# A graph network kernel on one core: 1,722 gathers of h rows are given the last row as a bound, with indices over it skipped

## The chip, the cores and the metric

The kernel runs on one core of one Trainium2 chip. The metric is the device time of one execution in microseconds (us). The time before the change is 3790.28 us, the median of two runs (3790.26 and 3790.29).

## What is computed

The input is x, 6250 nodes by 256 features, and 100,000 edges (src, dst) sorted by dst. Six graph layers are followed by a mix term and a mixture of eight experts:

```python
xn = _layernorm(x)
h = xn
for layer in range(6):
    agg = segment_sum(h[src], dst, num_segments=n)
    z = h + agg
    z = relu(batchnorm(z @ W1[layer] + b1[layer]))
    z = batchnorm(z @ W2[layer] + b2[layer])
    h = z if layer == 5 else relu(z)
x = x + h + mix(xn)
x = x + experts(_layernorm(x))
```

The step that matters here is `segment_sum(h[src], dst)`: for each node, the sum of the rows of h at the other ends of its edges.

## The kernel before, in words

The 6250 nodes are cut into 13 chunks by destination. The first 8 chunks (510 nodes each) are done densely: an adjacency matrix of edge counts, a "slab" of 49 tiles of 128 source nodes by 510 destinations, is multiplied with h, which stays in SBUF as two fp16 pieces (`PC`, named pieces). These are 8 x 196 matmuls a layer on TensorE at line 1181. The slabs are built in layer 0 and loaded again from memory by SyncE in each later layer.

The other 5 chunks are done sparsely, by "slots". A slot is 128 edges that follow one another in the sorted list. There are 287 of them (`NSLOT`). For each slot GpSimd issues one indirect DMA, a gather at line 1518: it takes 128 indices from one column of `SI` (named ssrc) and fetches 128 rows of 512 fp16 values, 1 KB each, from `d_H` (pieces_d), the copy of h in memory, into a buffer `SG` (sg0 to sg9, and from layer 1 on also sgm0 to sgm3). VectorE builds a one-hot matrix `SO` for the slot (line 1899), and TensorE multiplies gathered rows by it in 4 short matmuls (line 1217), which wait for the gather's semaphore `s_row` and the one-hot's `s_soh`. The last one counts up `s_smm`, and that frees the buffer. The indices in `SI` come from src with `min(N - 1)` applied (N is 6250), so none is over 6249.

The order of the work is written out ahead by `layer_order` and `side_work`: 1568 dense steps a layer, and at given steps a slot's matmuls. All engines follow the same list `ORDER[l]`, each for the items that concern it. Among the slots' matmuls stand mostly 5 dense matmuls. GpSimd runs ahead of TensorE: item `fetch_first` issues the first `lead_of(l)` gathers of the layer (8 in layer 0, 12 after it) once the writes of h to `d_H` have landed (`s_hst`), and each later gather j is issued in the order of slot j - `lead_of(l)`, after a wait on `s_smm` until its buffer, one of a ring of `ring_of(l)` (10 in layer 0, 14 after it), is free. GpSimd does nothing else while the gathers of layers 1 to 5 run. In layer 0 it also has a few operations for the slab keys among them.

After the last slot of a layer come the remaining dense steps, the statistics, the second matmul of the layer (lines 2067 and 2149), the scaling of h (line 1406) and its write to `d_H`, and the next layer's gathers. After layer 5 come the experts, with no such gathers.

The change touches `pool_layer` alone. Line 1076 (`pool_start`) holds ten other gathers of the same instruction, at the start of the program, three of them with 96 indices and seven with 128. The gathers inside `general` (line 2266) are for inputs that the fast path can't take, and don't run here.

Of the kernel before, what the change touches and what calls it, by code (L numbers as in the profile page):

```python
# [15 lines left out]
N = 6250  # L16
# [79 lines left out]
def ring_of(l):  # L96
    return RINGS + MORE if l else RINGS

def lead_of(l):  # L100
    return ring_of(l) - 2
# [197 lines left out]
def product_count(l, q, i, m):  # L299

    return gemm_count(l, q, i, m) - 2 * NCH * l
# [158 lines left out]
def build(nc, inp, cst, out):  # L460
# [33 lines left out]
    def small(name, shape, dt):  # L494
        return at(name, shape, dt, region(nbytes(shape, dt)))
# [11 lines left out]
    SI = small("ssrc", [P, 3 * SROWS], I32)  # L507
# [164 lines left out]
    def ring(name, k):  # L672
        return [nc.alloc_semaphore(f"{name}{i}") for i in range(k)]
# [15 lines left out]
    s_xin, s_xst, s_row = ring("s_xin", 4), ring("s_xst", 4), ring("s_row", RINGS + MORE)  # L689
# [360 lines left out]
    def pool_keys(w):  # L1050
        hi, lo = phl[w % 2][:, 0, :], phl[w % 2][:, 1, :]
        r, b, c, d = (pkt[j][:, :] for j in range(4))
        pool.wait_ge(s_bits, w)
        pool.wait_ge(s_kk, w + 2)
        pool.tensor_scalar(b, hi, float(WD), 1.0, ALU.mult, ALU.add)
        pool.tensor_scalar(r, GE_T[w][:, 0:256], wb5[:, w:w + 1], None, ALU.subtract).then_inc(s_pl, 1)
        pool.wait_ge(s_pl, pn())
        pool.tensor_scalar(c, r, 0.0, None, ALU.is_ge)
        pool.tensor_scalar(d, r, float(WD - 1), None, ALU.is_le)
        pool.tensor_tensor(b, b, r, ALU.add).then_inc(s_pl, 1)  # L1060
        pool.wait_ge(s_pl, pn())
        pool.tensor_scalar(r, lo, 1.0, None, ALU.add)
        pool.tensor_tensor(c, c, d, ALU.mult).then_inc(s_pl, 1)
        pool.wait_ge(s_pl, pn())
        pool.tensor_tensor(b, b, c, ALU.mult)
        pool.tensor_tensor(r, r, c, ALU.mult).then_inc(s_pl, 1)
        pool.wait_ge(s_pl, pn())
        pool.wait_ge(s_turn, w + 3)
        pool.tensor_tensor(pkk[:, 0, :], b[:, 0:P], b[:, P:2 * P], ALU.add)
        pool.tensor_tensor(pkk[:, 1, :], r[:, 0:P], r[:, P:2 * P], ALU.add).then_inc(s_kk, 1)  # L1070
# [327 lines left out]
    def pool_y(l):  # L1398
        pool.wait_ge(s_bn, norm_count(l - 1, 1))
        for g, (c, w) in enumerate(YG):  # L1400
            pool.wait_ge(s_gev, y_done(l, g))
            for m in range(2) if g else (1,):
                n = 2 * g + m
                if n >= YRING:
                    pool.wait_ge(s_ylo, 2 * len(YG) * (l - 1) + n - YRING + 1)
                pool.tensor_scalar(RY[n % YRING][:, 0:w], Z[:, m, c:c + w], scaled[:, m, 0:1], scaled[:, m, 1:2],  # L1406
                                   ALU.mult, ALU.add).then_inc(s_yf, 1)
# [91 lines left out]
    def pool_layer(l):  # L1499
        for item in ORDER[l]:  # L1500
            kind, i = item[0], item[1] if len(item) > 1 else None
            if kind == "bits":
                pool_keys(i)
            elif kind == "y" and i == 0:
                pool_y(l)
            elif kind == "fetch_first" or kind == "fetch":
                if kind == "fetch_first":
                    pool.wait_ge(s_hst, 16 * (9 + 14 * l))
                    if l == 0:
                        pool.wait_ge(s_keys, 4)  # L1510
                        pool.wait_ge(s_xst[3], 32)
                    else:
                        pool.wait_ge(s_gemm, product_count(l - 1, 1, NG2 - 1, 1))
                        pool.wait_ge(s_smm, NSLOT * l)
                for j in range(lead_of(l)) if kind == "fetch_first" else (i,):
                    if j >= ring_of(l):
                        pool.wait_ge(s_smm, NSLOT * l + j - ring_of(l) + 1)
                    pool.indirect_dma_start(out=SG[j % ring_of(l)][:, :], out_offset=None, in_=d_H[:, :],  # L1518
                                            in_offset=bass.IndirectOffsetOnAxis(ap=SI[:, j:j + 1], axis=0)
                                            ).then_inc(s_row[j % ring_of(l)], 16)  # L1520

    def sp_layer(l):
        for item in ORDER[l]:
# [1175 lines left out]
    def rest(any_edges):  # L2699

        for l in range(L):
            if l:
                pe_layer(l)
                act_layer(l, any_edges)
                dve_layer(l, any_edges)
                pool_layer(l)
                sp_layer(l)
            if any_edges:
                general(l)
            if l == L - 1:  # L2710
                sp_tail()
            pe_second(l)
            act_second(l, not any_edges)
            dve_second(l, not any_edges)
            pool_second(l)
        pe_ffn()
        act_ffn()
        dve_ffn()
        pool_ffn()
        sp_ffn()  # L2720
# [7 lines left out]
    act_layer(0)  # L2728
    dve_layer(0)
    pool_layer(0)  # L2730
    sp_layer(0)
    for engine in (pe, dve, act, pool, sp):
# [74 lines left out]
```

## Time and profile before

| | |
|---|---|
| runs | 3790.26 and 3790.29 us, median 3790.28 |
| the profiled execution, first to last instruction (its span) | 3784.5 us |
| runs over the span: what lies around it | 5.8 us |
| granted TensorE clock, mean | 0.997 |
| TensorE matmul busy | 96% |
| VectorE, ScalarE, GpSimd busy | 56%, 37%, 73% |
| gathers at line 1518 | 1,722 (6 x 287) |
| matmuls at line 1217 | 6,888 (4 for each gather) |

The profile gives no own time for the profiled execution beyond its span, so the 5.8 us are the runs' median less the span. PE is TensorE, DVE is VectorE, ACT is ScalarE, POOL is GpSimd, SP is SyncE. A gather's row on POOL lasts as long as POOL works on issuing it, and not until the rows have landed. Instructions of the sequencers (semaphores, registers) aren't counted as busy. "idle <-X" is time in which an engine did nothing, ended by X; "issue" means that nothing in the profile held it. A busy PE isn't PE at its peak, since matmuls overlap.

### The profile page before, as it was taken

How to read it: one execution, taken by the hardware profiler on the slowest of the kernel's cores; microseconds unless marked ns; L12 is line 12 of the kernel's file. 1: busy time of each engine (PE TensorE's matmuls, PEld its weight loads, DVE VectorE, ACT ScalarE, POOL GpSimd, SP SyncE). 2: the span in 40 equal slices, each digit the busy share in tenths (PEclk: the TensorE clock that was granted, in tenths of full speed). 3: DMA queues.
4: the chain of work that ended last, by engine and by line, in shares of the span. 5: the costliest groups of instructions: out<-in, count | busy, mean ns of one | idle time of the engine just before them, and what ended most of it. 6: DMA issues, size and time to landing. Idle time of an engine off the chain costs nothing.

```text
span 3784.5 us, 69343 instructions
## 1 busy us (share of the span) xinstructions
PE 3634.5 (96%) x26358; PEld 2033.4 (54%) x26358; DVE 2109.3 (56%) x6775; ACT 1416.3 (37%) x2665; POOL 2756.0 (73%) x2845
## 2 busy tenths in 40 slices
PE   2899999999999999999999999999999999999999
PEld 1455554544456555555555555555554555665666
DVE  9988775556465444732227222282223776777766
ACT  6666654200042000510006000060001767677777
POOL 5666664677756777667776677667776799999997
PEclk9999999999999999999999999999999999999999
DMA  6444342668525555255552565535554100000000
GB/s 205 144 127 151 124 151 84 204 220 273 177 100 185 190 173 172 90 186 192 193 182 95 170 207 181 169 128 189 190 177 126 63 22 12 23 12 23 11 16 10
DMA packets 203707, 506.19 MB, mean 134 GB/s; under 512 B 33860, under 2 KB 137872, under 8 KB 196848
## 3 DMA queue, kind: packets, MB, share of 16 engines
q0 software_dynamic: 83360, 227.95, 20.3%
q1 hardware_dynamic: 120016, 273.74, 19.9%
q8 instruction: 218, 3.57, 0.4%
q14 instruction: 113, 0.93, 0.1%
HBM read 412.08 MB, written 89.48 MB: 133 GB/s over the span
## 4 chain that ended last, share of the span: by engine, by line
PE 77%; DVE 9%; ACT 4%; DMA 4%; issue 3%; POOL 3%; SPq 0%; POOLq 0%; ACTq 0%; DVEq 0%
PE bank L1181 47%; PE bank L2428 6%; PE bank L2411 6%; PE bank L2396 5%; PE bank L1217 4%; PE bank L1293 3%; DMA sg<-pieces_d,ssrc 2%; PE bank L983 2%; DVE zh L2167 1%; ACT h L2467 1%; ACT f L2468 1%; DVE st L2192 1%; POOL sg L1518 1%; DVE ohk L782 1%; POOL ry L1406 1%
## 5 line engine op out<-in xcount | busy, mean ns | idle before, releaser
L1181 PE MATMUL bank<-slab,pieces 128*128 128x510 fp8e4 (+1 forms) x9408 | 2321.0, 378 | 5.3 <-DVE slab L801 5.3
L1518 POOL DMA_INDIRECT sg<-pieces_d,ssrc x1322 | 1261.7, 954 | 548.8 <-issue 249.4
L1181 PEld LDWEIGHTS bank<-slab,pieces 128*128 128x128 f16 (+1 forms) x9408 | 800.8, 97 | 668.2 <-DVE slab L801 7.7
L1899 DVE TENSOR_SCALAR so<-iota,skey 128x49 f16<-128x49 f16 (+21 forms) x1322 | 319.1, 262 | 599.5 <-PE bank L1217 598.2
L1423 ACT ACTIVATE z<-bank,prm,ct 128x510 f32<-128x510 f32 (+2 forms) x130 | 94.9, 749 | 1223.2 <-DVE st L1417 1223.2
L1217 PEld LDWEIGHTS bank<-so,sg 128*128 128x128 f16 x5288 | 322.1, 96 | 286.5 <-DMA sg<-pieces_d,ssrc 14.7
L1518 POOL DMA_INDIRECT sgm<-pieces_d,ssrc x400 | 380.7, 952 | 121.8 <-issue 90.8
L2686 POOL TENSOR_SCALAR btmp<-bob,rw 128x256 f32<-128x256 f32 (+1 forms) x343 | 400.3, 1167 | 33.5
L2467 ACT ACTIVATE h<-bank,fscale 128x512 f16<-128x512 f32 (+2 forms) x416 | 314.8, 757 | 186.4 <-PE bank L2411 186.1
L1217 PE MATMUL bank<-so,sg 128*128 128x51 f16 (+20 forms) x5288 | 343.2, 182 | 9.3 <-DMA sg<-pieces_d,ssrc 9.2
L930 ACT ACTIVATE slab<-bank 128x490 fp8e4<-128x490 f32 x408 | 278.4, 695 | 141.3 <-PE bank L983 138.1
L2468 ACT ACTIVATE f<-bank,fscale 128x512 f32<-128x512 f32 (+2 forms) x416 | 316.2, 760 | 0.0
L2689 POOL TENSOR_TENSOR mb<-mb,btmp 128x256 f32<-128x256 f32 (+1 forms) x343 | 279.6, 815 | 28.6
L2428 PE MATMUL bank<-fwo,h 128*128 128x256 f16 (+1 forms) x2352 | 277.9, 273 | 6.4 <-DVE h L2533 4.8
L2411 PE MATMUL bank<-h,fw 128*128 128x512 f16 (+2 forms) x1248 | 274.0, 367 | 6.6 <-ACT h L2467 3.8
L2396 PE MATMUL bank<-xp,fw 128*128 128x512 f16 (+2 forms) x1248 | 271.9, 366 | 0.3 <-ACT xp L2510 0.3
L983 PE MATMUL bank<-ohk,ohl 128*128 128x245 f16 x816 | 220.5, 284 | 44.7 <-ACT slab L930 33.5
L2428 PEld LDWEIGHTS bank<-fwo,h 128*128 128x128 f16 (+1 forms) x2352 | 227.1, 98 | 58.7 <-DVE h L2533 10.9
L782 DVE TENSOR_SCALAR ohk<-iota,keys 128x245 f16<-128x245 f16 x816 | 251.9, 311 | 0.0
L781 DVE TENSOR_SCALAR ohl<-iota,keys 128x128 f16<-128x128 f16 x816 | 228.1, 280 | 7.9 <-PE bank L983 4.8
L2533 DVE TENSOR_TENSOR h<-f,h 128x512 f16<-128x512 f32 (+2 forms) x208 | 145.8, 701 | 128.7 <-ACT f L2468 126.7
L1417 DVE BATCH_NORM_STATS2 st<-bank 128x6 f32<-128x510 f32 (+2 forms) x130 | 84.0, 662 | 229.4 <-PE bank L1181 136.9
(355 smaller groups left out, 3946.0 us busy)
## 6 DMA issues: line engine op xcount, KB each, us to landing
slab<-slabs SPq DMA_DIRECT2D x40, 3123.8 KB
pieces_d<-pieces SPq DMA_DIRECT2D x60, 512.0 KB
slabs<-slab SPq DMA_DIRECT2D x8, 3123.8 KB, 11.9
sg<-pieces_d,ssrc POOLq DMA_INDIRECT x1322
mx<-xnorm SPq DMA_DIRECT2D x24, 512.0 KB
ws<-L_ffn_W_dram SPq DMA_DIRECT2D x32, 256.0 KB, 8.1
sgm<-pieces_d,ssrc POOLq DMA_INDIRECT x400
experts<-wp SPq DMA_DIRECT2D x24, 256.0 KB, 4.1
```

The source lines that it names most:

```text
L782: dve.tensor_scalar(OHK[w % RING][:, 0:KW], iota[:, 0:KW], KL[:, 0, w:w + 1], None, ALU.is_equal).then_inc(s_oh, 1)
L983: pe.matmul(win_bank(pr)[:, KW * u:KW * u + KW], OHL[w % RING][:, :], OHK[w % RING][:, 0:KW], start=True, stop=True).then_inc(s_bmm, 1)
L1181: ins = pe.matmul(psD[half][:, 0:w], PC[:k, a, c:c + P], v[:k, a, :], start=(r == 0), stop=(r == 97))
L1217: ins = pe.matmul(psS(l)[half][:, lo:lo + w], SG[i % ring_of(l)][:, c:c + P], SO[i % ring_of(l)][:, 0:w], start=False, stop=True, skip_gro ...
L1518: pool.indirect_dma_start(out=SG[j % ring_of(l)][:, :], out_offset=None, in_=d_H[:, :], in_offset=bass.IndirectOffsetOnAxis(ap=SI[:, j:j + ...
L1899: dve.tensor_scalar(SO[j % ring_of(l)][:, 0:w], iota[:, 0:w], SK[:, j:j + 1], None, ALU.is_equal).then_inc(s_soh, 1)
L2396: ins = pe.matmul(psD[m][:, 0:n], fw1[:, e, k, pw, P * m:P * m + P], xps[c % 2][:, k, px, 0:n], start=(j == 0), stop=(j == 5))
L2411: ins = pe.matmul(psG[m][:, 0:n], fw2[:, e, k, pw, P * m:P * m + P], h1[:, k, px, 0:n], start=(j == 0), stop=(j == 5))
L2428: ins = pe.matmul(psB[pr][:kr, 256 * u:256 * u + 256], h2[:, k, px, P * (i0 + u):P * (i0 + u) + kr], fwo[:, e, k, pw, :], start=(j == 0), ...
L2467: act.activation(h[:, m, 0, 0:n], ps[m][:, 0:n], ACT.Relu, bias=b_, scale=s_).then_inc(s_h, 1)
L2468: act.activation(f[m][:, 0:n], ps[m][:, 0:n], ACT.Relu, bias=b_, scale=s_).then_inc(s_f, 1)
L2686: pool.tensor_scalar(btmp[:k, :], bob[e][:k, :], w_[:k, i, e:e + 1], None, ALU.mult).then_inc(s_pl, 1)
```

## The change

```diff
                     pool.indirect_dma_start(out=SG[j % ring_of(l)][:, :], out_offset=None, in_=d_H[:, :],
-                                            in_offset=bass.IndirectOffsetOnAxis(ap=SI[:, j:j + 1], axis=0)
-                                            ).then_inc(s_row[j % ring_of(l)], 16)
+                                            in_offset=bass.IndirectOffsetOnAxis(ap=SI[:, j:j + 1], axis=0),
+                                            bounds_check=N - 1, oob_is_err=False).then_inc(s_row[j % ring_of(l)], 16)
```

Each gather of line 1518 now names row 6249 as the last that may be read, and a row whose index is over it is left out of the transfer. No index is over it, so the same 128 rows are fetched. The list of instructions on each engine is the same before and after, row for row (PE 11830, DVE 10147, ACT 3092, POOL 5352, SP 628 rows). That list doesn't show register instructions.
## Rows read from the trace of the kernel before

**Rows 1.** The page: busy time of each engine, and the chain that ended last.
```profile
PE 3634.5 (96%) x26358; PEld 2033.4 (54%) x26358; DVE 2109.3 (56%) x6775; ACT 1416.3 (37%) x2665; POOL 2756.0 (73%) x2845
...
PE 77%; DVE 9%; ACT 4%; DMA 4%; issue 3%; POOL 3%; SPq 0%; POOLq 0%; ACTq 0%; DVEq 0%
```

**Rows 2.** Line 1518: durations (ns min/median/max), and POOL's idle time before it.
```profile
L1518 POOL DMA_INDIRECT sg<-pieces_d,ssrc x1322: 940/946/4613, 142.1 to 2905.7; - x189
L1518 POOL DMA_INDIRECT sgm<-pieces_d,ssrc x400: 942/946/1493, 713.3 to 2896.9; - x134
its engine sat idle before it (us, times) until:
  issue: 340.1, 1117
  PE bank L1217: 255.8, 600
  DMA pieces_d<-pieces: 74.7, 5
```

**Rows 3.** Timeline of POOL: first and last gathers of layer 0, then of layer 5.
```profile
142.12 1.09 POOL L1518 DMA_INDIRECT sg<-pieces_d,ssrc  x1 [0.16 <-issue]
...
573.77 0.94 POOL L1518 DMA_INDIRECT sg<-pieces_d,ssrc  x1 [0.31 <-issue]
...
2547.80 0.98 POOL L1518 DMA_INDIRECT sg<-pieces_d,ssrc  x1 [14.70 <-DMA pieces_d<-pieces]
...
2905.66 0.95 POOL L1518 DMA_INDIRECT sg<-pieces_d,ssrc  x1 [0.30 <-issue]
```

**Rows 4.** Timeline of PE in layer 5: the first and the last slot's matmuls.
```profile
2558.30 0.24 PE L1217 MATMUL bank<-so,sg 128*128 128x14 f16 x4
2558.41 1.24 PE L1181 MATMUL bank<-slab,pieces 128*128 128x510 fp8e4 x5
...
2916.42 0.25 PE L1217 MATMUL bank<-so,sg 128*128 128x32 f16 x4
2916.52 5.77 PE L1181 MATMUL bank<-slab,pieces 128*128 128x510 fp8e4 x26
```

**Rows 5.** Line 1518 in the gather stretches of layers 1 and 5: span, POOL busy (instructions).
```profile
700.00:1084.00 384.00, 274.88 (x287) 0.99 0.66 215
...
2547.00:2918.00 371.00, 271.67 (x287) 1.00 0.54 173
```

**Rows 6.** Line 1217, all layers: PE's idle time before it, by what ended it.
```profile
  DMA sg<-pieces_d,ssrc: 23.9, 21
  DMA sgm<-pieces_d,ssrc: 10.1, 9
```

**Rows 7.** Waits of POOL in layer 0 (142 to 700 us): total us, times, longest.
```profile
POOL sg L1518 <- PE bank L1217: 134.4, 220, 7.2
```

**Rows 8.** DMA issues of the page: a load from memory and its median time to landing.
```profile
mb<-mixed SPq DMA_DIRECT2D x10, 512.0 KB, 3.9
```

**Rows 9.** The chain that ended last, its longest DMA pieces in layers 2 and 5.
```profile
1210.73 10.82 DMA sg<-pieces_d,ssrc
...
2587.83 10.73 DMA sg<-pieces_d,ssrc
```

**Rows 10.** Waits of POOL in layer 5 (2547 to 2922 us): total us, times, longest.
```profile
POOL sg L1518 <- issue: 48.8, 160, 0.3
...
POOL sg L1518 <- PE bank L1217: 14.0, 46, 0.3
```

**Rows 11.** Timeline of POOL: two operations of which the second needs the first.
```profile
65.68 0.40 POOL L1055 TENSOR_SCALAR pkt<-phl 128x256 f32<-128x256 int32 x1 [4.38 <-DVE phl L790]
66.16 0.93 POOL L1056 TENSOR_SCALAR pkt<-ge,cf 128x256 f32<-128x256 int32 x1
```

**Rows 12.** Line 1076: gathers with 128 indices, and with 96 indices (ns min/median/max).
```profile
L1076 POOL DMA_INDIRECT ge<-edges_dram,cwi x7: 946/953/1160, 14.7 to 26.1; - x7
L1076 POOL DMA_INDIRECT ge<-slot_edges_dram,cwi x3: 909/912/926, 16.2 to 18.7; - x3
```

## The prediction

> **What bounds the kernel now.** I read the page first. PE is busy for 96% of the span and makes up 77% of the chain that ended last, and POOL is busy for 73% and makes up 3% of the chain [rows 1]. By that alone, some more work on POOL would be hidden. But these are averages over the program, so I next read the one line that the change touches. A gather keeps POOL busy for 0.946 us at the median, and before nearly each one POOL is idle: 1117 times for 340.1 us in all until "issue" (0.30 us each), 600 times for 255.8 us until PE's slot matmuls, and 5 times until the copy of h has landed, once in each of layers 1 to 5 [rows 2]. "Issue" says that nothing held POOL. So 0.95 + 0.30 = 1.25 us is what a gather costs POOL from start to start, and a gather that starts 1.25 us after the one before it was held up by nothing.
>
> The timeline shows where that is so. In layer 5 the first gather starts at 2547.80 and the last, the 287th, at 2905.66: 357.9 us for 286 steps, or 1.251 us a step [rows 3]. POOL never stops there. TensorE goes through the same slots at the same pace: from 2558.30 to 2916.42 is 358.1 us, or 1.252 us a slot [rows 4]. Two engines with one pace, and POOL's pace is its own cost. Layers 1 to 5 are alike, 287 gathers each in 384 us (layer 1) to 371 us (layer 5) [rows 5]; layer 1 is the loosest, by 13 us. The order gives PE mostly 5 dense matmuls and a slot's 4 per slot. PE hardly waits for the gathers: 23.9 + 10.1 = 34 us over all layers [rows 6]. So in this stretch PE is busy, but only just: POOL is 100% taken with no reserve beyond what is in flight. In layer 0 it is otherwise. Its gathers take from 142.12 to 573.77, 431.7 us or 1.509 us a step [rows 3], and POOL waits 134.4 us for buffers [rows 7], so PE sets the pace there and POOL has 1.509 - 1.25 = 0.26 us to spare per gather.
>
> How much is in flight: the first gather of layer 5 ends at 2548.78 and its matmuls start at 2558.30, 9.5 us later. The last ends at 2906.61 and is used at 2916.42, 9.8 us later [rows 3, 4]. Part of that is the landing. The trace has no landing time for gathers by itself. A 512 KB load lands in 3.9 us [rows 8], and a gather moves 128 KB, so I take 4 us for a common one; but in each of layers 2 to 5 the chain runs once through a gather that took over 10 us to land (10.82 and 10.73 in layers 2 and 5 [rows 9]), and leaves no reserve there. The reserve s is thus between 0 and 9.8 - 4 = 5.8 us. I take 5, since a late landing must fall near the layer's end to take it away.
>
> **The change, part by part.** It removes and moves nothing, and adds two things to each of 1,722 gathers. Say they cost POOL d us per gather together. Then the last gather of a layer comes 286 d later, its slot waits for it, and behind that slot are only 26 dense matmuls, 5.77 us [rows 4], before the layer's statistics. PE works in order, so the layer grows by 286 d - s. Nothing gives it back: the next layer's h, its copy to memory and its gathers all start from this end. Over layers 1 to 5 that is 5 (286 d - s).
>
> First, the register write. It sits on POOL's sequencer ahead of the gather. It costs nothing if the sequencer does it while the gather before is still being worked on. For that speaks that in layer 5 the idle time is the same whether it is ended by "issue" (48.8 us over 160, 0.30) or by the matmul that frees the buffer (14.0 over 46, 0.30) [rows 10]. Against it speaks the same 0.30 us: between dependent ordinary operations POOL loses only 66.16 - 66.08 = 0.08 us [rows 11], so something in a gather's start doesn't overlap. The ends are 0 and 0.30 (a whole second start of a gather), nearest is the 0.08 of the hand-over, and I take 0.05.
>
> Second, the test of 128 indices against the bound. Without a test, 128 indices take 0.953 us and 96 take 0.912 [rows 12]: 0.041 us for 32, or 1.3 ns an index, and 0.79 us are fixed. All that is done for an index today (reading it, making an address, writing it out) costs 128 x 1.3 = 0.16 us. A compare and a choice beside it in the same manner should be under that: I take 0.07. The lower end is 0, or a little below, if the instruction takes a shorter path with a bound. The upper end is where the test is made index by index in a path of its own; as the nearest row I take a whole gather again, 0.95 us.
>
> So d = 0.05 + 0.07 = 0.12 us. Layers 1 to 5: 5 x (34.3 - 5) = 147 us; layer 1's 13 us of slack could take up to that off, which I leave to the range. Layer 0: 1.25 + 0.12 is under 1.509, nothing. The experts have no gathers, nothing. Span 3784.5 + 147 = 3931.5, and with the 5.8 us around it 3937 us, against a median of 3790.28: 3.9% slower. A change of 2%, 76 us, is about what a measurement of this kernel can tell from none. It is reached at 286 d = 15.2 + 5, so at d = 0.07 us. That is little, and whether each small cost is hidden decides the sign of the verdict.
>
> The idle time of 0.30 us before a gather with nothing holding it is the row; one rule speaks against my reading of it. The Trainium skill, "DMA: Bandwidth & Descriptors", section "Anatomy of one DMA", puts a DMA's fixed cost mostly on the confirmation of the write, says of descriptor generation that "you can emit a lot of descriptors before the incremental cost shows up", and gives the sequencer about 50 ns. By it, work added at the issue would be small and the latency hidden by early issue, and the time would stay near the old. Only this case's pace speaks for the other side; "Perfetto Trace Analysis", section "What 'DMA-bound' means", names just this, a sequencer solid with DMA slices, and the trace agrees with 0.95 of each 1.25 us.
>
> **The rivals.** (a) Hidden: the register write falls under the gather ahead of it, and the test runs beside the fixed 0.79 us. For it: only 1.3 ns an index show today, and the constant 0.30 us. Against it: it must hold for both costs to within 0.07 us on an engine that never rests for 358 us. Time: 3790, with up to 3866 where part shows. That also covers that the bound isn't looked at on the chip at all. This is the case on the other side: not slower by 2%, with d = 0.07 us as its point.
>
> (b) Index by index: the test, or the leaving out of rows that it must provide for, forces a slower path. At d = 0.4 layers 1 to 5 give 5 x (114.4 - 5) = 547 us. Layer 0 gets slower too: 1.65 us against 1.509 are 286 x 0.141 = 40 us, less the 9.8 us in flight, 30. Time 3790 + 577 = 4367. At d = 0.95 it is 5 x 266.7 + 286 x 0.69 - 10 = 1521, so 5311. For it speaks that 0.79 us of a gather are fixed, which looks like work done for all indices at once, and that can break. Against it: nothing in the rows of before.
>
> (c) Faster: the path with a bound is shorter. PE could then win no more than its waits for gathers, 34 us [rows 6]: 3756, within 2%. Nothing speaks for it.
>
> **How the numbers follow.** The forecast, d from 0.07 to 0.3, has 0.47, and its own range is 3866 to 5 x (85.8 - 5) = 404 over, 4194. Case (a) has 0.31, (b) 0.18, (c) 0.04. Slower by over 2%: 0.47 + 0.18 = 0.65. Within 2%: 0.34. Faster by over 2%: 0.01. The point is the forecast's, 3937. For 8 in 10 the range must reach into (a) to its end and into (b) to its beginning: 3786 to 4367. Beyond lies some 0.04 below and 0.14 above.
>
> **What would show it.** In the profile after, the median of line 1518 should be 0.946 + 0.07 us, and the idle time until "issue" 0.30 + 0.05 us; which of the two grew tells the parts apart. In layer 5 the step from gather to gather should be 1.37 us and PE's step from slot to slot the same. PE's idle time before line 1217 until the gathers should grow from 34 us by about what the span grows. The first and last gather of layer 0 should stand as far apart as before. I am wrong if the gather takes 0.95 us and the idle time stays 0.30 (then a), if the gather takes over 1.25 us (then b), or if both grow as said and the span doesn't: then the reserve s was far more than 5 us, and PE's pace wasn't tied to POOL's.

## The result, and the profile after

The changed kernel takes 3847.9 us (two runs, 3846.3 and 3849.5) against 3790.3: a ratio of 1.0148 (95% interval 1.0131 to 1.0164), 57.6 us or 1.5% slower. Four more runs on another chip gave 3844.1 against 3792.7, a ratio of 1.0137 (1.0119 to 1.0155). The kernel got slower, as forecast, but by 58 us where I had said 147. That is a true loss, clear of the interval, but under the 2% that I called visible and 89 us less than I had said: on size the forecast was wrong. The profiled execution's span is 3842.4 us, 57.9 more than before.

Line 1518 of the changed kernel (durations in ns min/median/max, then POOL's idle time before it), which answers to [rows 2]:

```profile
L1518 POOLq MOVE  x1722: 29/29/35, 140.7 to 2958.2; - x192
L1518 POOL DMA_INDIRECT sg<-pieces_d,ssrc x1322: 992/998/2036, 141.7 to 2968.2; - x189
L1518 POOL DMA_INDIRECT sgm<-pieces_d,ssrc x400: 994/998/1244, 714.0 to 2959.1; - x134
its engine sat idle before it (us, times) until:
  issue: 397.5, 1284
  PE bank L1217: 187.5, 433
  DMA pieces_d<-pieces: 76.6, 5
```

The gather grew from a median of 0.946 to 0.998 us. The 1722 register writes stand on POOL's sequencer with 29 ns each, and the idle time until "issue" is still 397.5/1284 = 0.31 us (before 340.1/1117 = 0.30). So the register write doesn't lengthen the step. The test does, by 0.052 us. The register writes run far ahead of their gathers here: the last one starts at 2958.2 and its gather at 2968.19, 10 us later. The waits put down to buffers fell from 600 to 433, but most of that is bookkeeping, because the wait now stands on the register write. With the wait on the gather, in the run with one register write a layer below, they are 557.

The timeline of POOL in the changed kernel: the first gather of layer 1, then the first and last of layer 5.

```profile
700.88 1.06 POOL L1518 DMA_INDIRECT sg<-pieces_d,ssrc  x1 [15.76 <-DMA pieces_d<-pieces]
...
2595.23 1.05 POOL L1518 DMA_INDIRECT sg<-pieces_d,ssrc  x1 [15.20 <-DMA pieces_d<-pieces]
...
2968.19 1.00 POOL L1518 DMA_INDIRECT sg<-pieces_d,ssrc  x1 [0.30 <-issue]
```

The timeline of PE there, the first and the last slot of layer 5:

```profile
2605.24 0.24 PE L1217 MATMUL bank<-so,sg 128*128 128x14 f16 x4
...
2974.27 0.25 PE L1217 MATMUL bank<-so,sg 128*128 128x32 f16 x4
2974.37 7.93 PE L1181 MATMUL bank<-slab,pieces 128*128 128x510 fp8e4 x36
```

And in the kernel before, the first gather of layer 1:

```profile
700.82 0.98 POOL L1518 DMA_INDIRECT sg<-pieces_d,ssrc  x1 [15.26 <-DMA pieces_d<-pieces]
```

These rows show where the time went. Until layer 1 begins, nothing is lost (700.88 against 700.82), though layer 0 has a sixth of the gathers. From there to the first gather of layer 5 are 1894.4 us, and were 1847.0 ([rows 3] has 2547.80): 47.4 us more for four layers, 11.8 a layer. From that gather to layer 5's last slot are 379.0 us, and were 368.6 [rows 3, 4]: 10.4 more. Together 57.8 of the 57.9 us. POOL's step in layer 5 is (2968.19 - 2595.23)/286 = 1.304 us, before 1.251: longer by 0.053, the growth of the gather. The last gather now ends 5.1 us ahead of its matmuls (2969.19 to 2974.27), where it was 9.8. POOL's 286 steps take 373.0 us where they took 357.9: 15.1 us of delay, less 4.7 us of reserve used up, are the layer's 10.4.

These rows also set right what stands behind a layer's last slot. [rows 4] shows 26 dense matmuls and 5.77 us there only because its window ended; in both kernels it is 36 matmuls and 7.93 us. No term of the sum hangs on it.

PE's waits ahead of line 1217 in the changed kernel (total us, times, longest):

```profile
PE bank L1217 <- DMA sg<-pieces_d,ssrc: 35.4, 28, 2.7
PE bank L1217 <- DMA sgm<-pieces_d,ssrc: 20.9, 14, 3.2
```

And in the kernel before:

```profile
PE bank L1217 <- DMA sg<-pieces_d,ssrc: 9.2, 10, 2.1
PE bank L1217 <- DMA sgm<-pieces_d,ssrc: 3.9, 3, 1.9
```

They grew by 43.2 us; about the rest of the 57.9 us stands as busy time of matmuls whose ends are modelled (PE busy 3634.5 before, 3651.3 after). The number of waits tells more than the sum. PE doesn't wait at each slot but 42 times in all. The chain that ended last shows which gathers it waits for; these are its longest DMA pieces in layer 5 of the changed kernel:

```profile
2634.36 11.02 DMA sg<-pieces_d,ssrc
2687.77 11.65 DMA sg<-pieces_d,ssrc
2735.05 11.03 DMA sg<-pieces_d,ssrc
2787.14 10.99 DMA sg<-pieces_d,ssrc
2836.65 11.45 DMA sg<-pieces_d,ssrc
2886.15 10.10 DMA sgm<-pieces_d,ssrc
```

Before, the chain had one such piece in the layer [rows 9], now it has six, some 50 us apart. Those are the gathers that PE waits for. Something else in the trace comes at the same six times: SyncE's loads of the next slab from memory. The loads of layer 5 in the changed kernel, then in the kernel before (ns min/median/max, first and last start), and the size of one:

```profile
L1532 SPq DMA_DIRECT2D slab<-slabs x6: 332/335/451, 2633.5 to 2884.8; - x6
...
L1532 SPq DMA_DIRECT2D slab<-slabs x6: 332/335/451, 2586.5 to 2830.0; - x6
...
slab<-slabs SPq DMA_DIRECT2D x1, 3123.8 KB
```

In the changed kernel they are issued at 2633.5, 2685.7, 2733.8, 2786.1, 2835.8 and 2884.8, each 0.9 to 2.1 us ahead of one of the six pieces. That the two share the DMA engines and so slow each other is the natural reading; no run moved a load to show it. The change didn't make the landings later. By the trace's semaphore events for each gather (worked out from the packed trace, no view prints them), the median gather of layer 5 lands 2.78 us after its start before and 2.85 after, longer only by what the gather itself grew. 30 gathers before and 29 after take over 8 us, in six groups in both kernels.

So late landings were there before, and most of them fell within the reserve. Now POOL is later each time, and at each of them the delay gathered since the last one is paid. Counted from the first gather of layer 5, PE's slots in the changed kernel are behind those of the kernel before by 1.7 us at slot 40, 5.4 at slot 120, 7.4 at slot 200 and 10.4 at slot 240 and from there to the end; between the late landings the lag stands still. The last of the six comes at 2886, the 223rd step of the layer, when POOL is 223 x 0.053 = 11.8 us late. What POOL loses behind it is covered by the common reserve.

### The profile page after: what moved, and what is told of

Same layout as the page of the kernel before. It is cut to its first block, busy times and chain, and to the rows that moved or that the text cites. A ratio compares the mean times of both kernels' runs of the same rounds, so it can differ in the third digit from the quotient of the medians.

```text
span 3842.4 us, 71065 instructions
## 1 busy us (share of the span) xinstructions
PE 3651.3 (95%) x26358; PEld 2034.1 (53%) x26358; DVE 2107.7 (55%) x6775; ACT 1416.2 (37%) x2665; POOL 2843.8 (74%) x2845
## 4 chain that ended last, share of the span: by engine, by line
PE 73%; DVE 8%; DMA 7%; ACT 4%; issue 4%; POOL 3%; POOLq 0%; SPq 0%; ACTq 0%; DVEq 0%
PE bank L1181 44%; PE bank L2428 6%; PE bank L2411 6%; PE bank L2396 5%; DMA sg<-pieces_d,ssrc 5%; PE bank L1217 4%; PE bank L1293 3%; DMA sgm<-pieces_d,ssrc 2%; PE bank L983 2%; DVE zh L2167 1%; ACT h L2467 1%; ACT f L2468 1%; DVE st L2192 1%; DVE ohk L782 1%; POOL sg L1518 1%
## 5 line engine op out<-in xcount | busy, mean ns | idle before, releaser
L1518 POOL DMA_INDIRECT sg<-pieces_d,ssrc x1322 | 1329.5, 1006 | 539.7 <-issue 311.6
L1518 POOL DMA_INDIRECT sgm<-pieces_d,ssrc x400 | 401.2, 1003 | 121.9 <-issue 86.0
## 6 DMA issues: line engine op xcount, KB each, us to landing
slabs<-slab SPq DMA_DIRECT2D x8, 3123.8 KB, 11.5
```

## The experiments

Twelve runs. The first four ran on a chip where the kernel before takes 4151.4 us and TensorE is idle for long stretches until its own issue; the others on chips where it takes 3790 to 3793 us. Each ratio is against the kernel before on the same chip. Each run says which part of the change it undid or did alone.

**One register write a layer, bound kept.** The register is written once a layer; all else is the changed kernel.

```diff
     def pool_layer(l):
+        last_row = pool.snap(pool.to_reg(N - 1))
...
-                                            bounds_check=N - 1, oob_is_err=False)
+                                            bounds_check=last_row, oob_is_err=False)
```

First run: 

> The bound stays on all 1722 gathers of line 1518, but its register is written once a layer and not once a gather. Theory (the test itself costs 0.05 us in the gather's own time, the register write is hidden, since the idle time before a gather stayed 0.30 us): the gather stays at 0.998 us, its idle time at 0.30 us, and the time stays where the changed kernel's is, 3847.9 us, within 3 us. Rival (the register write, 29 ns in the trace, is part of the price): the step from gather to gather falls by 0.03 us or so, and the time by 5 x 286 x 0.029 = 41 us, to about 3806 us.

Measured: 4144.3 against 4151.4 us, ratio 0.9984 (0.9974 to 0.9994). The gather took 1.002 us, and yet nothing was lost. Neither number expected came, since on this chip something else sets the pace. PE's and POOL's longest waits there (total us, times, longest):

```profile
POOL sg L1519 <- PE bank L1217: 327.4, 294, 8.4
...
PEld bank L1181 <- issue: 234.8, 422, 2.4
PE bank L1181 <- issue: 107.9, 215, 2.0
...
PE bank L1217 <- issue: 76.1, 145, 1.9
```

TensorE waits for its own instructions, and POOL waits 327 us for TensorE to free buffers. Most likely the 0.05 us of a gather come out of that wait; no trace of the kernel before on this chip shows it. So the run shows that the test need not cost time, but not yet what the register write costs where POOL sets the pace.

Second run, on a chip at 3793 us: 

> The bound on all gathers with one register write a layer, again. With the kernel before at about 3790 us: the theory that the gather's own 0.052 us is the price says a ratio of 1.015, as for the changed kernel beside it; the theory that the register writes are the price says 1.000. With the kernel before at about 4150 us: again about 0.998.

Measured: 3843.0 against 3792.7 us, ratio 1.0134 (1.0116 to 1.0152); the changed kernel beside it 1.0137. The gather took 0.998 us. Within what these runs can tell apart (some 7 us), the test alone makes the whole loss. The trace shows one small price of the register writes. Here POOL's waits for the copy of h, ahead of the first gather of layers 1 to 5, are

```profile
  DMA pieces_d<-pieces: 74.0, 5
```

and 76.6 us in the changed kernel: 0.5 us more at each, 15.20 in place of 14.67 us in layer 5.

**The changed kernel again**, beside it. 

> The changed kernel itself, to have it beside the others on their chip. If TensorE isn't held up by its own issue there (kernel before at about 3790 us): ratio 1.015, as on record. If it is, as in the four runs before this (kernel before at 4151 us, TensorE idle for 190 us until issue ahead of line 1217): theory one (the price is the gather's 0.05 us, and is free where POOL waits for buffers) says a ratio within 0.3% of 1, as the kernel with one register a layer had (0.9984). Theory two (1722 more instructions in POOL's stream cost TensorE instruction supply on such a chip) says 1.015, as the run in error mode had.

Measured: 3844.1 us, ratio 1.0137 (1.0119 to 1.0155), with the gather at 0.998 us.

**More instructions for the sequencer, no bound.** The kernel before with

```diff
+                    for _ in range(4):
+                        pool.wait_ge(s_const, 32)
                     pool.indirect_dma_start(out=SG[j % ring_of(l)][:, :], out_offset=None, in_=d_H[:, :],
```

> The kernel before, with no bound, and four waits that are long satisfied ahead of each gather, which the program packs into two more sequencer instructions each. They make POOL's stream longer than the register write does (two instructions against one) and leave the gather alone. Theory one: gather 0.946 us, idle time before it at 0.30 us, and 3790 us within 8 us, since the sequencer does them while the gather ahead is being worked on. Rival (each sequencer instruction shows): 0.04 us or more for each, idle time 0.38 us, time 3790 + 5 x (286 x 0.08 - 4) = 3884 us. On a chip at 4150 us theory two says 1.03.

Measured: 3791.2 us, ratio 0.9996 (0.9987 to 1.0006). The gather stayed at 0.946 us and the idle time until issue at 0.30. The added sequencer instructions (3450, two for each gather) and line 1520 of this run:

```profile
L1519 POOLq EVENT_SEMAPHORE  x3450: 17/43/43, 141.8 to 2902.1; - x192
...
L1520 POOL DMA_INDIRECT sg<-pieces_d,ssrc x1322: 940/946/1961, 142.9 to 2908.4; - x189
...
  issue: 333.5, 1095
```

Two more sequencer instructions ahead of each gather are hidden. With the run of one register write a layer, that settles the first term: it was 0 in the step.

**The bound in layer 0 alone**, and on the ten gathers at the start.

```diff
...
-                                            bounds_check=N - 1, oob_is_err=False)
+                                            **({} if l else dict(bounds_check=N - 1, oob_is_err=False)))
```

First run, on the chip at 4151 us: 

> The bound stays on the 287 gathers of layer 0 alone, and is given to the ten gathers at the start (line 1076) too. Theory (only layers 1 to 5 are paced by POOL): the gathers of layer 0 take 0.05 us more each, 14 us of POOL's time in all, and the kernel's time is 3790 us, within 3 us; only waits of POOL for buffers in layer 0 get shorter. Rival (POOL's time costs in every layer alike): 57.6 / 6 = 10 us, 3800 us. At line 1076: if the test costs per index, the three gathers with 96 indices grow by three quarters of what the seven with 128 grow (0.039 against 0.052 us); if it costs per gather, both grow by 0.052 us.

Measured: 4162.5 us, ratio 1.0030 (1.0019 to 1.0041): a small loss that my theory doesn't give (more on it in the last section). Second run: 

> The bound on the gathers of layer 0 and of the start alone, again, now hopefully on a chip where the kernel before takes 3790 us. Theory (only where POOL sets the pace does the 0.052 us count): 3790 us, ratio 1.000 within 0.2%. Rival (every bounded gather costs alike, a sixth of 1.4%): ratio 1.0023, 3799 us.

Measured: 3790.2 against 3790.7 us, ratio 1.0001 (0.9991 to 1.0011). The 287 gathers of layer 0 were each longer, and the kernel wasn't. POOL's waits in layer 0, here and then in the kernel before, where those for buffers are 134.4 us [rows 7]:

```profile
POOL sg L1518 <- issue: 79.8, 237, 1.4
POOL sg L1518 <- PE bank L1217: 63.4, 50, 6.8
...
POOL sg L1518 <- issue: 20.3, 67, 0.3
```

Only the sum of both can be compared, since the wait for a buffer now stands on the register write and is partly put down to issue. It fell from 154.7 to 143.2 us, by 11.5, where 287 x 0.052 = 15: the longer gathers came out of POOL's idle time.

**The price by number of indices.** At line 1076 of this last run (ns min/median/max):

```profile
L1076 POOL DMA_INDIRECT ge<-edges_dram,cwi x7: 994/1004/1222, 15.7 to 27.6; - x7
L1076 POOL DMA_INDIRECT ge<-slot_edges_dram,cwi x3: 952/953/971, 17.2 to 19.8; - x3
```

Against [rows 12], 128 indices cost 0.051 us more (0.953 to 1.004) and 96 cost 0.041 more (0.912 to 0.953). The 128 are a weak witness here: in the changed kernel, where these ten gathers have no bound, the median of the seven is 1.013 us too, since more of them take over 1.0 us, for a reason that stays open. The shortest of the seven is 0.946 us in both kernels without a bound here, and 0.994 with one. A run of its own had smaller ones:

```diff
     def pool_start():
+        for _ in range(3):
+            pool.indirect_dma_start(**trial(16)).then_inc(s_trial, 16)
+            pool.indirect_dma_start(**trial(16, bounds_check=b, oob_is_err=False)).then_inc(s_trial, 16)
...
+            pool.indirect_dma_start(**trial(128, bounds_check=b, oob_is_err=False)).then_inc(s_trial, 16)
+            pool.indirect_dma_start(**trial(128, bounds_check=0, oob_is_err=False)).then_inc(s_trial, 16)
```

> The kernel before, with 21 gathers more at the start, each waited for, three each of: 16, 64 and 128 indices without and with a bound, and 128 indices with row 0 as the bound, so that all but those with index 0 are left out. If the test costs per index: with less without is 0.006, 0.026 and 0.052 us. If it costs per gather: 0.052 us at each size. With nearly all rows left out: the gather on POOL takes the same 0.998 us if the work is done for every index whatever the outcome, and less if a row left out saves the writing of its descriptors; its landing, read from the start of the next gather, should be earlier by what 128 rows take to move.

Measured (one run, 4225.1 us, on the chip at 4151), in the order 16, 64, 128 indices, without and with a bound, and last 128 with all left out but those of index 0:

```profile
L1083 POOL DMA_INDIRECT ge<-edges_dram,cwi x3: 876/878/1056, 15.2 to 63.4; - x3
L1084 POOL DMA_INDIRECT ge<-edges_dram,cwi x3: 901/901/911, 19.9 to 66.6; - x3
L1085 POOL DMA_INDIRECT ge<-edges_dram,cwi x3: 927/933/937, 22.6 to 69.3; - x3
L1086 POOL DMA_INDIRECT ge<-edges_dram,cwi x3: 960/960/960, 27.6 to 72.9; - x3
L1087 POOL DMA_INDIRECT ge<-edges_dram,cwi x3: 959/962/967, 30.7 to 76.0; - x3
L1088 POOL DMA_INDIRECT ge<-edges_dram,cwi x3: 1022/1025/1037, 34.7 to 80.0; - x3
L1089 POOL DMA_INDIRECT ge<-edges_dram,cwi x3: 1002/1002/1006, 38.2 to 83.6; - x3
```

The bound costs 0.023, 0.027 and 0.063 us at 16, 64 and 128 indices. Neither pure form holds, as far as three gathers each can show: some 0.02 us are there with few indices, and the rest grows with them. Leaving nearly all rows out saves POOL only 0.023 us (1.025 to 1.002). It makes the landing earlier, as expected: by the semaphore events, 1.31 to 1.44 us after the gather's end in place of 2.21 to 2.34.

**Error in place of skip.**

```diff
-                                            bounds_check=N - 1, oob_is_err=False)
+                                            bounds_check=N - 1, oob_is_err=True)
```

First run, at 4151 us: 

> The bound stays on all gathers of line 1518, but an index over it is an error and not skipped. Theory A (having a bound costs): gather 0.998 us, time 3848 us. Theory B (leaving rows out costs, since descriptors must be dropped): gather 0.946 us or between, time 3790 us or between. I lean to A by 2 to 1.

Measured: 4219.9 us, ratio 1.0154 (1.0137 to 1.0171), gather 1.012 us. Second run: 

> The bound on all gathers with an index over it as an error, again, for a chip at 3790 us. On the slower chip its gather took 1.012 us against 1.002 in skip mode. Theory: d = 1.008 - 0.946 = 0.062 to 0.066 us, so 3790 + 5 x (286 x 0.064 - 4) = 3861 us, ratio 1.019. Rival (the modes are alike in price): 1.0137.

Measured: 3867.6 against 3790.7 us, ratio 1.0204 (1.0187 to 1.0221), gather at 1.012 us:

```profile
L1518 POOL DMA_INDIRECT sg<-pieces_d,ssrc x1322: 1006/1012/1980, 141.2 to 2986.8; - x189
```

So skipping isn't the dear part: the error mode costs 0.014 us a gather more. It serves as a second dose: d = 0.066 us gives 77 us, where d = 0.052 gives 51 on such chips. The difference is 26 us where 5 x 286 x 0.014 = 20. With some 6 us of uncertainty on each time, that agrees with the rule of 286 us a layer for each us of d.

**A dose without any bound.** The kernel before with a tiny operation ahead of each gather of layers 1 to 5:

```diff
...
+                    if l:
+                        pool.wait_ge(s_pl, own["p"])
+                        pool.memset(spare[:, :], 0.0).then_inc(s_pl, 1)
+                        pn()
                     pool.indirect_dma_start(out=SG[j % ring_of(l)][:, :], out_offset=None, in_=d_H[:, :],
```

> The kernel before, without a bound, with one tiny operation of GpSimd (a memset of one column) ahead of each of the 1435 gathers of layers 1 to 5. It leaves indices, DMAs and registers alone and only lengthens the step from gather to gather, by d, which the trace will give (I expect 0.1 to 0.4 us). Theory: the time is 3790 + 5 x (286 d - 4), with the 4 us of reserve that the changed kernel showed: 3913 us at d = 0.1, 4199 at d = 0.3. Rival (something else than POOL's pace made the 57 us): the time stays near 3790 us, or doesn't follow 286 d.

Measured: 3802.1 against 3790.7 us, ratio 1.0034 (1.0020 to 1.0049). I had expected a larger d. The timeline of POOL says why:

```profile
2559.78 0.99 POOL L1523 DMA_INDIRECT sg<-pieces_d,ssrc  x1
2560.77 0.12 POOL L1521 MEMSET spare<- 128x1 f32 x1
2561.08 0.95 POOL L1523 DMA_INDIRECT sg<-pieces_d,ssrc  x1 [0.19 <-issue]
...
2922.53 0.11 POOL L1521 MEMSET spare<- 128x1 f32 x1
2922.84 0.95 POOL L1523 DMA_INDIRECT sg<-pieces_d,ssrc  x1 [0.19 <-issue]
```

The memset takes 0.12 us and stands in the 0.30 us that were idle. The step is (2922.84 - 2559.78)/286 = 1.2694 us, 0.018 more than before. With the 4 us of reserve that I had put in, the rule gives 3796 us for that. From the measured 11.5 us, 5 x (5.2 - s), s is 2.9. Three doses, one of them with no bound, thus lie near one line: d of 0.018, 0.052 and 0.066 us cost 2.3, 10.3 and 15.4 us a layer, which are 286 d less 2.9, 4.6 and 3.5 us. It is the step from gather to gather that costs, whether a bound or a memset makes it longer.

**Slots placed later, in the changed kernel.**

```diff
-        g0, g1 = 75, STEPS * NDC - 36
+        g0, g1 = 95, STEPS * NDC - 16
```

> The changed kernel with the slots of layers 1 to 5 placed 20 dense steps later in the order (first from step 75 to 95, last from 36 steps before the end to 16). Theory: POOL gets 20 x 0.216 = 4.3 us more of lead over TensorE in each of five layers, and where POOL sets the pace the layer's loss of 10 to 12 us falls by that: 3848 - 21 = 3827 us beside a kernel before at 3790. If the loss doesn't come from POOL's pace, the shift changes nothing (3848). On a chip at 4150 us, nothing either way.

Measured: 3837.9 us, ratio 1.0113 (1.0095 to 1.0131), 6 us less than the changed kernel beside it and not 21. All four runs lie below all four of the changed kernel, so the direction is right. In layer 5 the first slot starts 14.3 us after the first gather, where it was 10.0, as meant. But the last slot starts 380.2 us after it, where it was 379.0. The lead is lost again at the late landings, as POOL's step is still 1.303 us, and only 16 dense steps in place of 36 are left behind that slot. I had left out both. How the gain of 6 us is made up of them wasn't worked out.

**The same in the kernel before, by 8 steps** (83 and 28 in place of 75 and 36). 

> The kernel before with the slots of layers 1 to 5 placed 8 dense steps later (first from step 75 to 83, last from 36 before the end to 28). It tries for a version better than both: TensorE waits 13 us for gathers' rows ahead of its matmuls in the kernel before, and 8 x 0.216 = 1.7 us more lead should take about half of it away, while the shift by 20 in the changed kernel showed that a shorter tail costs some 2 us a layer. I expect 3785 to 3795 us, ratio 0.998 to 1.001.

Measured: 3782.6 against 3790.7 us, ratio 0.9981 (0.9972 to 0.9991), faster than both kernels, and 2 us below the range that I had given. PE's waits for gathers are down to 10.1 us from 13.1:

```profile
PE bank L1217 <- DMA sg<-pieces_d,ssrc: 6.0, 5, 2.1
PE bank L1217 <- DMA sgm<-pieces_d,ssrc: 4.1, 2, 3.0
```

That is 3 us and not half of the 13, and the kernel gained 8. Where the other 5 come from stays open.

## Why the prediction was right or wrong

The step that failed is the size of d, what the change adds to POOL's step from gather to gather: 0.05 + 0.07 = 0.12 us in the sum, 0.052 measured. The path from there to the time held.

- **"POOL is 100% taken with no reserve beyond what is in flight"**: right. 0.052 us on an engine that the page shows at 73%, 3% of the chain, cost 1.5% of the time. The run with the bound in layer 0 alone and the run with the memset show it from both sides. The prediction also named this "a sequencer solid with DMA slices". That fits less well: 0.95 of each 1.25 us is 76% of POOL, not solid, and POOL's sequencer was up to 10 us ahead. The sign to go by was the equal step on both engines.
- **The register write, "I take 0.05"**: wrong, it was 0 in the step. One write a layer gave 1.0134 beside 1.0137, and two instructions more gave 0.9996. My reading of the 0.30 us, "so something in a gather's start doesn't overlap", was true of the gather, but I charged it to the sequencer. Its next instructions do run beside the gathers ahead, and most of a small memset's time fits into the 0.30 us too. The Trainium skill, "DMA: Bandwidth & Descriptors", section "Anatomy of one DMA", gives about 50 ns to the sequencer's dispatch of a DMA. No run here times that dispatch by itself; the register write, another instruction, has 29 ns in the trace.
- **The test, "I take 0.07"**: right in kind, 0.052 us measured. The bound by slope, 128 x 1.3 = 0.16 us for all that is done for the indices, held, though the slope was read too steep: the gathers with 128 indices in [rows 12] also fetch rows twice as long as those with 96. In the run by sizes, with equal rows, 16 to 128 indices took 0.878 to 0.962 us, 0.75 ns an index. Case (b), a path index by index, fell.
- **Layer 0 costs nothing, 5 x (286 d - s)**: right in form, and s came out at 2.9 to 4.7 us where I had 5. With d = 0.052 my own formula gives 5 x (14.9 - 5) = 49 us, 3840 us. The miss is the size of d: 0.12 against 0.052 us, and 286 x 5 = 1430 times that difference is 97 us, of which the smaller s gives some 8 back. Of the two terms the register write's 0.05 us makes 72 us and the test's excess of 0.018 the rest.
- **Layer 1's 13 us of slack**: it took nothing off. From its first gather to its last slot layer 1 grew by 12.2 us (382.1 to 394.3), no less than the others. POOL's step grew there as in the others, from 1.280 to 1.334 us, so the slack wasn't POOL's to use.
- **The landing, "I take 4 us for a common one"**, by a load of 512 KB: it was 2.8 us (by the semaphore events). With it the reserve of a common gather is 7 us. That 5 us was still near the truth for s is partly luck: it is set by the landings of over 10 us, of which the last comes at the 223rd gather.
- **"leaves no reserve there"** of slow landings, and then "a late landing must fall near the layer's end": half right. Such landings come every 50 us in both kernels, with each slab load, and each takes its part of the delay. I saw one a layer, since the others fell within the reserve and so weren't on the chain.
- **What would show it**: the idle time should have grown by 0.05 and didn't, the gather by 0.07 and did by 0.052. That is between what I had forecast and case (a), and the point I named for a 2% loss, d = 0.07 us, wasn't reached. PE's step did follow POOL's, from 1.252 to 1.290 us beside 1.251 to 1.304, less the reserve used up. PE's idle time by the row I had named grew from 34 to 137 us and not by what the span grew.
- **My waits of 34 us** summed weight loads and matmuls, which wait side by side; so does the row of 137. PE's own were 13.1 and 56.3 us, so the bound on any gain in (c) was less than I wrote.

## What to carry to other kernels

Before pricing something that is done once per DMA, compare the pace of the issuing engine with that of its consumer, stretch by stretch. Where both have the same step, as in layers 1 to 5 here, a cost of 0.05 us repeated 1430 times goes straight into the time, less a few us of lead. Where the issuing engine waits for buffers, as in layer 0, it was free. One or two sequencer instructions ahead of each gather cost nothing while gathers were queued ahead of them, so look for the price in the instruction's own duration first. And look at what else lands at the moments when the consumer waits: here each costly landing came with a 3.1 MB load. A bound that no index can break isn't free protection; clamping the indices once, as this kernel does, made it needless.

## What the runs showed of the hardware

- An indirect DMA with a bound held POOL 0.998 us for 128 indices against 0.946 without; with an error in place of a skip 1.012. Leaving out all rows but those of index 0 saved 0.023 us of POOL's time.
- A memset of 0.12 us, put into the 0.30 us between two gathers, lengthened the step by only 0.018 us.
- Where a gather really has to wait, a wait that stands on the register write costs 0.5 us more than one on the gather. In the run by sizes each gather waits for the landing of the one before. By the semaphore events, a gather that waits itself starts 0.26 us after that landing. Where the wait stands on a register write, the write starts 0.02 us after the landing and the gather 0.78 to 0.84 us after it. Such gathers follow one without a bound in that run, but that isn't the cause: the landing of 16 rows comes 1.43 to 1.56 us after the gather's end with and without a bound, leaving aside the first gather of all. The 0.5 us at each layer's first gather in the changed kernel are the same thing. The rows of POOL's timeline (line 1084 has a register write ahead of it, line 1085 none):

```profile
44.03 0.90 POOL L1084 DMA_INDIRECT ge<-edges_dram,cwi  x1 [2.23 <-DMA ge<-edges_dram,cwi]
46.67 0.93 POOL L1085 DMA_INDIRECT ge<-edges_dram,cwi  x1 [1.74 <-DMA ge<-edges_dram,cwi]
...
66.61 0.90 POOL L1084 DMA_INDIRECT ge<-edges_dram,cwi  x1 [2.31 <-DMA ge<-edges_dram,cwi]
69.33 0.93 POOL L1085 DMA_INDIRECT ge<-edges_dram,cwi  x1 [1.82 <-DMA ge<-edges_dram,cwi]
```

- One chip took 4151 us for the kernel that takes 3790 on others. Its granted clock was 0.975 to 0.989, and TensorE waited on its own issue (107.9 us ahead of line 1181 and 76.1 ahead of line 1217 in the run with one register write a layer; on the other chips neither wait is among its longest). What makes it so was not looked into.
- On that chip the run in error mode with 1722 register writes lost 1.54%, that with 297 lost 0.30%, and that with one a layer lost nothing, though POOL waited for buffers in all of them. The losses go with the number of register writes in POOL's stream (297/1722 x 1.54% = 0.27%). That would be a second price that shows only there. It stays open: the changed kernel itself didn't run on that chip, and the run in error mode differs from that with one register write in two things.
